# A three-stage transformer kernel on one core: its hardware loop over tiles written out pass by pass, and a one-column matmul ahead of two products left out

## The reference

```python
x = x + attn_b(cond_a(x, bias, mask))       # a: attention, 16 heads of 64, one shared key/value head, a null key
                                            # b: gated linear scan over the 64 tokens, projections of 512, residual
x = x + ffn(cond2_c(x, mask))               # c: attention with normed queries and keys and a position bias,
                                            #    then a mixture of 8 experts with the best one chosen (argmax)
```

```python
attn = softmax(where(mask, q @ k.T + bias, neg))
out  = (attn @ v).reshape(b, n, 1024) @ Wo
```

## Time and profile before

| | |
|---|---|
| three runs | 1855.22, 1854.79, 1848.14 us |
| median | 1854.79 us |
| span of the profiled execution, first to last instruction | 1852.3 us |
| median less span | 2.5 us |
| instructions in the span, all kinds | 38642 |
| PE busy | 1661.7 us, 90% |
| DVE / ACT / POOL busy | 62% / 50% / 46% |

### The profile page before, as it was taken

The page is one execution under the profiler, slowest core; times in us unless marked ns, Lnnn a source line. Parts: engine busy times, 40 slices in busy tenths (PEclk is TensorE's granted clock), DMA queues, the critical chain, the costliest instruction groups (busy, mean ns, idle before and its releaser), DMA issues.

```text
span 1852.3 us, 38642 instructions
## 1 busy us (share of the span) xinstructions
PE 1661.7 (90%) x11791; PEld 1285.1 (69%) x11791; DVE 1149.3 (62%) x2536; ACT 918.0 (50%) x2231; POOL 849.6 (46%) x552
## 2 busy tenths in 40 slices
PE   2248999999999999999999999999999999999775
PEld 2136777777777777777777777777777777777653
DVE  2465666666667666676666666666666666766432
ACT  0224555555554555555555555555545555555421
POOL 1024545555444455554444455554444555545431
PEclk9579999999999999999999999999999999999986
DMA  7110000000000000000000000000000000000000
GB/s 219 52 29 7 2 10 10 10 0 9 9 9 9 9 9 9 3 6 9 9 9 9 9 9 9 0 9 9 9 9 9 9 9 4 5 9 7 7 4 6
DMA packets 40234, 26.57 MB, mean 14 GB/s; under 512 B 19826, under 2 KB 38274, under 8 KB 40196
## 3 DMA queue, kind: packets, MB, share of 16 engines
q1 hardware_dynamic: 40196, 26.09, 5.4%
HBM read 21.37 MB, written 4.71 MB: 14 GB/s over the span
## 4 chain that ended last, share of the span: by engine, by line
PE 81%; DVE 8%; issue 5%; ACT 3%; SPq 2%; POOL 1%; DVEq 0%; DMA 0%; POOLq 0%; ACTq 0%
PE bank L742 13%; PE bank L679 13%; PE bank L707 7%; PE bank L819 6%; PE bank L633 6%; PE bank L635 5%; PE bank L634 5%; PE bank L734 4%; PE bank L720 4%; PE bank L808 3%; PE bank L834 3%; PE bank L663 2%; DVE a_sum L1264 2%; SPq L455 2%; PE bank L799 1%
## 5 line engine op out<-in xcount | busy, mean ns | idle before, releaser
L1624 POOL TENSOR_TENSOR y<-y,u 128x512 f32<-128x512 f32 x128 | 162.7, 1271 | 47.3 <-DVE u L1357 42.1
L1604 POOL TENSOR_TENSOR resid<-xres,a_c 128x256 f32<-128x256 f32 x32 | 23.3, 727 | 346.5 <-DVE x L1365 346.5
L1616 POOL TENSOR_TENSOR u<-xe,Ef 128x512 f32<-128x512 f32 x96 | 122.7, 1292 | 42.8 <-ACT Ef L1092 42.8
L679 PEld LDWEIGHTS bank<-a_xnT,a_wq 128*128 128x128 f32 x1024 | 126.8, 195 | 17.1 <-issue 14.1
L819 PE MATMUL bank<-u,Gm 128*128 128x512 f32 x256 | 130.1, 611 | 4.7 <-DVE Gm L1349 3.8
L633 PE MATMUL bank<-w_e_hi,cT_hi 128*128 128x512 f32 x256 | 122.5, 478 | 10.2 <-DVE c_c L1413 10.2
L679 PE MATMUL bank<-a_xnT,a_wq 128*128 128x128 f32 x1024 | 127.5, 279 | 0.0
L742 PEld LDWEIGHTS bank<-a_wo,a_prob 128*128 128x128 f32 x512 | 96.0, 192 | 43.9 <-ACT a_prob L995 31.8
L1585 POOL TENSOR_TENSOR a_prob<-a_prob,a_mask 128x1024 f32<-128x1024 f32 x32 | 75.6, 2363 | 109.0 <-DVE a_prob L1235 109.0
L679 PE MATMUL bank<-c_xnT,c_wq 128*128 128x128 f32 x1024 | 125.4, 282 | 0.0
L742 PE MATMUL bank<-a_wo,a_prob 128*128 128x256 f32 x512 | 120.0, 388 | 5.4 <-ACT a_prob L995 3.4
(11 more groups left out here) (294 smaller groups left out, 4427.5 us busy)
## 6 DMA issues: line engine op xcount, KB each, us to landing
a_xin<-in_x SPq DMA_DIRECT2D x32, 128.0 KB, 2.4
xres<-in_x SPq DMA_DIRECT2D x32, 128.0 KB, 2.6
out<-acc SPq DMA_DIRECT2D x32, 128.0 KB, 1.7
a_wq<-in_L_cond_Wq SPq DMA_DIRECT2D x1, 1024.0 KB, 5.4
a_wo<-in_L_cond_Wo SPq DMA_DIRECT2D x1, 1024.0 KB, 6.5
c_wq<-in_L_cond_Wq SPq DMA_DIRECT2D x1, 1024.0 KB
c_wo<-in_L_cond_Wout SPq DMA_DIRECT2D x1, 1024.0 KB
u<-in_L_ffn_expert_w SPq DMA_DIRECT2D x3, 256.0 KB, 4.0
```

The lines of the kernel that those rows point to most:

```text
L679: mm = pe.matmul(bank(f"q{half}")[:, m * P:(m + 1) * P], X.wq[:, k, hp * P:(hp + 1) * P], X.xnT[:, k, :], start=k == 0, stop=k == KD - 1)
L1616: pool.tensor_tensor(u[l][:, :], xi[:, :], (E0u if l == 0 else Ef[l])[:, :], ALU.mult)\
L1624: pool.tensor_tensor(y[:, :], y[:, :], tm[l][:, :], ALU.add).then_inc(g.done(f"y{l}"), 1)
```

## The change

Two edits. `iterations` loses its loop: all 37 passes are written out, so t is a plain number in each and every wait has a constant. And `PV` loses the one-column matmul. Nothing else differs; the lines of the changed kernel stand 1 to 6 lower.

```diff
-LOOP_FROM = MAX_LAG + 1
...
-            for i in range(LOOP_FROM):
+            for i in range(NT + MAX_LAG):
                 if before and i in before:
                     before[i]()
-                run(i)
-            with eng.Fori(LOOP_FROM, NT) as i:
-                run(i)
-            for i in range(NT, NT + MAX_LAG):
                 run(i)
...
                     pe.wait_ge(*act.at("PT1", t))
-                    pe.matmul(bank("O0")[0:DH, 0:1], X.V[0:32, 0, :], X.PT[0:32, 0, 0:1], start=True, stop=True)
```

## The result

| | before | changed |
|---|---|---|
| median | 1854.72 us, 4 runs | 1822.61 us, 4 runs |
| lowest to highest | 1848.14 to 1855.22 | 1821.07 to 1824.77 |
| span of the profiled execution | 1852.3 us | 1819.1 us |
| mean granted clock of PE | 0.966 | 0.97 |

The ratio is 0.984, with a 95% interval of 0.9821 to 0.986. The forecast was 1831, with a range of 1821 to 1841: the direction and the mechanism hold, the gain is 32.1 us where 23.8 were forecast. Nearly all of the surplus lies outside the passes that the sum was made from.

A forecast was written before the change was run, and what follows sets the result against it. PE was taken to set the pace, busy 90%, with short detours through DVE and ACT. Writing out the loop (18.4 us) and dropping c's one-column matmul (5.4) gave 23.8 us off 1854.79: 1831.0 us, range 1821 to 1841.

The forecast's parts named there:

- Pass 5 as the sample of a written-out pass: Pass 5, already written out, takes 51.73 us against 52.44 in the loop; over 26 passes 18.4 us less.
- The matmul of c: One-column matmul ahead of c's quarter products in c.O, on the path: 0.17 us a tile, 5.4 us over 32 tiles.
- The rival in which the drain is paid at the products anyway: Quarter products gain nothing from dropping the one-column matmul; time 1836.4 us, chance 0.08.
- The matmul of a: One-column matmul in a.O, covered by ACT's back-to-back work until a.W: counted as 0.
- Where in the pass the 0.72 lies: Pass 5 against a loop pass, cut at PE's waits: 0.19, 0.10 and 0.44 less, 0.03 more, 0.02 less.
- POOL's loop worth nothing: POOL's own register instructions are worth nothing, since passes 5 and 32 agree up to L775.
- Fetching the longer lists at 0: Some 3 instruction packets for PE in each of 26 passes, 1.1 us each, hidden behind work and counted at 0.
- stall of 0.31 us a packet: Rival that fetches stall PE: from 0.31 us a packet the change turns slower; at 1.1 us, 1917; chance 0.04.
- The rival in which the loop had paid a fetch a pass: Each taken loop branch forced a fetch, so the gain grows by 29 us, to 1802 us; chance 0.02.
- The sum: 18.4 us for the loop plus 5.4 for c's matmul, 23.8 us off: 1831.0 us; chance 0.74, own range 1827 to 1836.
- the rival in which a.O counts too: a.O's 0.17 us also counts if ACT's run up to 762.31 is shortened; time 1825.6 us, chance 0.07.
- the margin for scatter: About 5 us on either side of the matmul's bounds 1825.6 and 1836.4, since runs of before differ by 7.

## Why the prediction was right, and where it was short

**Pass 5 as the sample of a written-out pass: right.** The forecast was 18.4 us over 26 passes; with both one-column matmuls kept the 26 passes take 1344.64 us, 18.8 less. Reading one pass of the old kernel that already was what the new one would be gave this to half a microsecond.

**The matmul of c: right, a little small.** The forecast was 0.17 us a tile, and 0.20 was measured (1344.64 less 1339.53, over 26). Going straight from full-array matmuls to quarters costs nothing more than going to 32 rows did: from the start of the full-array matmul ahead of c.O to the start of what follows are 0.55 us either way (766.91 to 767.46 us with both matmuls kept, 762.59 to 763.14 in the changed kernel). The term took the distance between the starts of the two matmuls. The rival in which the drain is paid at the products anyway falls.

**The matmul of a: right.** 0.00 measured, for the reason given: ACT's unbroken run ahead of a.W. One sentence on what the profile would show was wrong. I wrote that b.G to the first product of c would stay at 10.8; it is 10.98, because the mark b.G stands behind a.O and moved 0.2 forward against a.W, which didn't.

**Where in the pass the 0.72 lies: right by place, wrong for PE.** The forecast gave 0.19 us of it to the three register instructions of PE in front of c.O, and the 0.10 and 0.44 up to L849 and L775 to the lists of DVE and ACT. The loop put back on PE alone costs 0.03; DVE's costs 0.54, ACT's 0.09. The 0.19 at c.O is real but is recovered before the pass ends. That the total came out right owes nothing to this division: it was the length of pass 5 as a whole. Subtracting stretch by stretch shows where a difference arises, not that it lasts.

**POOL's loop worth nothing: right**, 0.01 with SP's. **Fetching the longer lists at 0: right.** From 340 to 1640 us the queues now show

```profile
q8 instruction: 75, 1.23, 0.4%
q14 instruction: 51, 0.42, 0.1%
```

three packets of PE's in each of 25 passes, as forecast, and the passes take 51.50 to 51.68 us. No stall of 0.31 us a packet has room in that. The rival in which the loop had paid a fetch a pass falls too: it asked for 1.1 us a pass more, and the passes now written out are as long as pass 5.

**The sum: short by 8 us.** The median lies nearest the rival in which a.O counts too (1825.6), which the runs refute. What was missing is time outside the 26 passes. Of the 33.2 us between the two profiled spans, 23.5 lie in the passes 6 to 31. 3.8 lie ahead of them (288.17 against 291.96) and 5.9 behind (191.04 against 196.92), where the forecast had 1 us for six tiles. The code there is that of before but for the one-column matmuls. The clock is not steady there. Of each pair of rows below the first is the start and the second the tail. In the changed kernel:

```profile
0.00:288.17 288.17, 185.77 (x1310) 143.74 (x1311) 155.32 (x354) 109.62 (x270) 97.25 (x65) 0.88 0.19 51
1628.06:1819.10 191.04, 148.56 (x890) 108.82 (x889) 89.99 (x206) 68.98 (x168) 70.98 (x46) 0.90 0.02 6
```

and in the kernel before:

```profile
0.00:291.96 291.96, 189.31 (x1325) 147.42 (x1326) 155.42 (x355) 109.87 (x270) 97.47 (x65) 0.87 0.19 50
1655.38:1852.30 196.92, 154.70 (x900) 114.00 (x898) 89.67 (x206) 68.91 (x168) 70.52 (x46) 0.87 0.02 6
```

The granted clock of the tail (the column before DMA share) goes with its length: 0.87 and 196.92 us before, 0.90 and 191.04 after. In the nine kernels with the same table of orders the start ran from 288.2 to 292.6 us, in no clear order by edit, and the kernel before alone had runs from 1846.84 to 1856.96 us in one comparison: scatter of this size exists. But the tails do fall in an order. In the five kernels without c's one-column matmul they took 189.1 to 191.4 us; in the four that have it 191.9 and 195.2 written out, and 196.9 and 197.9 in the two in which PE loops. That is one profile each, and the kernel with a.xn ahead of c.K, which has neither that matmul nor a loop, took 194.7.

The medians leave it open too. Taken from its own comparison, the gain in the median less the gain in passes 6 to 31 is 8.6 us for the changed kernel, 0.2 to 3.6 for six others with the same orders, and 5.1 below zero for the loop on PE. So the steady gain of 23.5 us is shown, and the cause of the surplus stays open: scatter of the start and tail can make it, and a part that belongs to the edits, through PE's clock in the tail, is not excluded. The forecast counted 1 us for these parts; that the median still fell within its range, by 1.6 us, is owed to the margin for scatter and is in part luck.

## What to carry to other kernels

A kernel that writes out its first and last passes around a loop holds its own forecast: compare a full written-out pass with a looped one, with the same counts of instructions, before costing anything by hand. Time taken off an engine on the path can be lost again at its next wait; look there for whether the partner started from this engine's work (c.O, kept) or has long been running (a.O, lost). Before shortening instructions, look for one that lasts several times its usual length, and at what runs on the other engine beside it: moving one step in DVE's order was worth more than both edits together.

## What the runs showed of the hardware

- A hardware loop's register instructions were dearest on DVE: 0.54 us a pass for 102 of them, against 0.09 for ACT's 82 and 0.03 for PE's 71 (each from one profile, with differences of up to 0.02 between kernels that should agree). These are costs in this kernel, where PE waits for DVE in each pass, and not costs of an instruction.
- An fp32 `tensor_scalar` from SBUF to SBUF of 256 columns takes 0.41 us alone and 1.99 us when a GpSimd `tensor_tensor` of 1.95 us began 0.11 us ahead of it. `qss`, read from PSUM, took 0.29 us beside the same GpSimd instruction.
- The tail of this pipeline, where PE is less busy (79% busy before and 78% after, against 97% in passes 6 to 31), ran at a granted clock of 0.86 to 0.92, the passes before it at 1.00. Five kernels with the same PE work in it, but for the matmul of a in one, took 189.1 to 191.4 us for it.
- On queue q8 three instruction packets came per pass of 51.5 us when all passes were written out, and the passes were as long as pass 5; in the loop of before none came from 352 to 1660 us.
